# A graph attention kernel: one mask product in 16 bits, one product for three values an edge, and window tables with two buffers

## The reference, cut to what matters

```python
# x: (6250, 96) f32; src, dst: (200000,) int32, sorted by dst
q = (x[src] @ qW).reshape(e, 4, 24)
k = (x[dst] @ kW).reshape(e, 4, 24)
v = (x[dst] @ vW).reshape(e, 4, 24)
exp_s = exp(clip(sum(q * k, -1), -10, 10))
norms = segment_sum(exp_s, src)[src]
res = segment_sum((exp_s / (norms + 1e-8))[:, :, None] * v, src)
out = layernorm(x + (x + res))
```

## Time and profile before

| | |
|---|---|
| Median of 3 runs | 1709.44 us (1707.88 to 1710.03) |
| Profiled execution | 1711.48 us, its span 1709.3 us |
| Mean granted TensorE clock | 0.936 |
| Busy share of the span | PE 87%, VectorE (DVE) 86%, ScalarE (ACT) 74%, GpSimd (POOL) 59% |
| DMA | 465.03 MB, 272 GB/s over the span |
| Setup, first phase, second phase | to about 140, to about 856, to the end |

### The profile page before, as it was taken

The page is one execution under the profiler, slowest core; times in us unless marked ns, Lnnn a source line. Parts: engine busy times, 40 slices in busy tenths (PEclk is TensorE's granted clock), DMA queues, the critical chain, the costliest instruction groups (busy, mean ns, idle before and its releaser), DMA issues.

```text
span 1709.3 us, 56067 instructions
## 1 busy us (share of the span) xinstructions
PE 1482.0 (87%) x19964; PEld 1425.5 (83%) x19965; DVE 1469.3 (86%) x2980; ACT 1265.3 (74%) x1844; POOL 1016.7 (59%) x764
## 2 busy tenths in 40 slices
PE   4873988888888988888769999999999999999990
PEld 3652878888788878887759999999999999999990
DVE  6988998898988998898158999999999999999987
ACT  2341665565666666665559999999999999999984
POOL 6230776777777776777725555555555555555551
PEclk8566999999999999999979999999999999999995
DMA  5673899999999999999897777777777777777732
GB/s 155 225 276 132 312 370 337 336 346 366 348 352 343 341 367 339 357 339 344 333 302 257 238 238 241 244 238 239 239 243 242 237 240 240 243 239 237 240 113 56
DMA packets 159451, 465.03 MB, mean 272 GB/s; under 512 B 36994, under 2 KB 59266, under 8 KB 152244
## 3 DMA queue, kind: packets, MB, share of 16 engines
q1 hardware_dynamic: 123572, 301.16, 54.1%
q0 software_dynamic: 35840, 163.36, 23.9%
HBM read 271.21 MB, written 209.73 MB: 281 GB/s over the span
## 4 chain that ended last, share of the span: by engine, by line
PE 80%; DVE 8%; issue 6%; DMA 2%; SPq 2%; ACT 1%; POOL 0%; DVEq 0%; POOLq 0%; ACTq 0%
PE two_a L1131 14%; PE two_b L1131 13%; PE meta L1193 12%; PE sum_bank L1193 12%; PE two_a L1214 7%; PE two_b L1214 7%; PE one_d L1204 3%; PE one_c L1204 3%; PE meta L1149 2%; PE one_d L1160 2%; DMA work<-kv_table 1%; PE sum_bank L1113 1%; SPq L825 1%; DVE acc L1614 1%; DVE cols_work L1315 1%
## 5 line engine op out<-in xcount | busy, mean ns | idle before, releaser
L698 POOL TENSOR_TENSOR work<-work 128x768 f32<-128x768 f32 x236 | 450.8, 1910 | 357.4 <-ACT work L939 357.4
L635 POOL DMA_INDIRECT sorted_rows<-work x448 | 501.3, 1119 | 215.2 <-issue 215.2
L948 ACT ACTIVATE work<-work 128x1024 f32<-128x1024 bf16 x236 | 500.8, 2122 | 0.0
L1131 PE MATMUL two_a<-work 128*128 128x192 bf16 x2688 | 268.5, 251 | 86.8 <-issue 84.3
L903 ACT ACTIVATE work<-two_a 128x768 f32<-128x768 f32 x224 | 181.5, 810 | 187.0 <-PE two_a L1131 186.2
L1131 PEld LDWEIGHTS two_a<-work 128*128 128x128 f16 x2688 | 220.0, 100 | 107.5 <-issue 89.0
L1131 PE MATMUL two_b<-work 128*128 128x192 bf16 x2688 | 267.5, 251 | 0.0
L1193 PE MATMUL meta<-work 128*128 128x100 f32 x1888 | 236.1, 278 | 0.8 <-DVE acc L1548 0.8
L1193 PE MATMUL sum_bank<-work 128*128 128x100 f32 x1888 | 235.2, 278 | 0.0
L1579 DVE TENSOR_REDUCE work<-work 128x32 f32<-128x768 f32 x236 | 225.0, 953 | 8.2
L1131 PEld LDWEIGHTS two_b<-work 128*128 128x128 f16 x2688 | 225.9, 100 | 6.8
(11 more groups left out here) (229 smaller groups left out, 2211.8 us busy)
## 6 DMA issues: line engine op xcount, KB each, us to landing
work<-sorted_rows SPq DMA_DIRECT2D x472, 392.0 KB, 3.5
work<-sorted_local SPq DMA_DIRECT2D x56, 1024.0 KB
sorted_rows<-pad_rows SPq DMA_DIRECT2D x49, 392.0 KB, 4.5
work<-kv_table SPq DMA_DIRECT2D x112, 144.0 KB
sorted_rows<-work POOLq DMA_INDIRECT x448
kv_table<-work SPq DMA_DIRECT2D x12, 576.0 KB, 3.4
work<-in_x SPq DMA_DIRECT2D x12, 192.0 KB, 3.8
sorted_local<-work SPq DMA_DIRECT2D x56, 8.0 KB
```

The costliest lines, as they stand in the source:

```text
L635: pool.indirect_dma_start(out=rows_dram, out_offset=bass.IndirectOffsetOnAxis(ap=place_now[:, p, u, b:b + 1], axis=0), in_=payload[:, p, u ...
L698: pool.tensor_tensor(now[:, :, 0:D].rearrange("p c (h f) -> p c h f", h=HEADS), blk[:, k, :, :, D:2 * D].rearrange("p m c (h f) -> p (m c) ...
L948: act.activation(hot_f[:, k % HOTF], hot[:, k % HOTS].rearrange("p n c -> p c n"), ACT.Copy).then_inc(hotf_made[k % PSEM], 1)
L1131: mm = pe.matmul(to, picked[:, u % 2, k * P:(k + 1) * P], window[:, u, :, n, :], start=(n == 0), stop=(n == 2))
```

## The change

Three parts, in the functions of the first phase and of the setup.

1. **The mask.** ScalarE copies `slots` out of PSUM to 16 bits, spread to pairs (`slots_h`, 200 elements a partition), after its two copies of b and ahead of the copy of the turned targets. VectorE makes `masked` with one product of 1400 elements, both inputs 16 bits in SBUF. TensorE's next `first_slots` waits for ScalarE's copy, not for the mask.
2. **The values.** Three values an edge, not four: `src_tag`, `dst_hi`, `dst_lo`, held beside each other (`held`), and one product of 1344 elements makes `vals`. `dst_local` goes: the setup subtracts the base from the target itself, and the low part is the local target where the targets of a group span less than 128. The sort's products have 48 columns. The slow branch, not taken when every group's targets lie within one window, adds the base (`base_f`) back.
3. **The windows.** `window` has two buffers of both groups, and one semaphore for each buffer. The sync queue, at the head of each iteration, waits until `kv` of c - 1 is over for both groups and loads both windows for c + 1.

```diff
+        held = cols_work[:, 1:1 + NV, :] ... "p (g v c) -> p g v c", v=NV, c=HC)
+        src_tag, dst_hi, dst_lo = (held[:, :, v, :].rearrange("p (g h) c -> p g h c", h=HB) for v in range(NV))
-        window, at = share(at, [QUAD, 2, 3, D], BF16)
+        window, at = share(at, [2, QUAD, 2, 3, D], BF16)
# SyncE
-            def window_of(u, lo, at_c):
-                group_done(sp, kv_made[KPARTS - 1], u, at_c)
-                sp.dma_start(window[:, u].rearrange("p x a b -> p (x a b)"), kv3[bass.ds(lo, P), :]
-                             ).then_inc(window_in[u], 16)
+            def windows(los, p):
+                for u in range(QUAD):
+                    sp.dma_start(window[:, p, u].rearrange("p x a b -> p (x a b)"), kv3[bass.ds(los[u], P), :]
+                                 ).then_inc(window_in[p], 16)
 
             def emit(a, b, c, p=None):
+                if c is not None and (not isinstance(c, int) or c + 1 < NQ):
+                    p = parity(c, p)
+                    los, at_c = bases(plus(sp, c, 1)), counts(sp, c, G2, 0)
                     for u in range(QUAD):
-                        window_of(u, los[u], {})
+                        group_done(sp, kv_made[KPARTS - 1], u, at_c, 1)
+                    windows(los, 1 - p)
                 if b is not None:
                     ... (write local targets)
-                if c is not None and following:
-                    window_of(0, los[0], at_c)
                     ... (broadcast brow)
-                if c is not None and following:
-                    for u in range(1, QUAD):
-                        window_of(u, los[u], at_c)
# ScalarE
+                if a is not None:
+                    act.wait_ge(slots_made, plus(act, a, 1))
+                    if not zero(a):
+                        act.wait_ge(masked_made, a)
+                    act.activation(slots_h, slots.unsqueeze(3).to_broadcast([P, QUAD, NB, HC]), ACT.Copy
+                                   ).then_inc(slots_kept, 1)
# TensorE
-                    pe.wait_ge(window_in[u], c16)
+                    if u == 0:
+                        pe.wait_ge(window_in[p], loaded)
-                        pe.wait_ge(masked_made, times(pe, a, QUAD))
+                        pe.wait_ge(slots_kept, a)
# VectorE, setup
-            link(dve.tensor_tensor(dst_local, dcol_i, base_ps.unsqueeze(2).to_broadcast([P, NG, COLS]), ALU.subtract))
+            link(dve.tensor_tensor(dcol_i, dcol_i, base_ps.unsqueeze(2).to_broadcast([P, NG, COLS]), ALU.subtract))
+            link(dve.tensor_copy(base_f[:], base_ps))
-                link(dve.tensor_copy(dst_hi, bits))
+                link(dve.tensor_copy(dst_hi, pairs))
# VectorE, first phase
-                    for v, held in enumerate((src_tag, dst_hi, dst_lo, dst_local)):
-                        dve.tensor_tensor(vals[:, :, v], onej, quad_of(held, a).unsqueeze(2)
-                                          .to_broadcast([P, GH, NCH, HC]), ALU.mult).then_inc(vals_made, 1)
+                    dve.tensor_tensor(vals, onej.unsqueeze(2).to_broadcast([P, GH, NV, NCH, HC]),
+                                      held[:, bass.ds(times(dve, a, GH), GH)].unsqueeze(3)
+                                      .to_broadcast([P, GH, NV, NCH, HC]), ALU.mult).then_inc(vals_made, 1)
-                def mask(u):
-                    if u == 0:
-                        dve.wait_ge(slots_made, a1)
-                    dve.tensor_tensor(masked[:, HB * u:HB * (u + 1)], hits[:, 0, u],
-                                      slots[:, u, :].unsqueeze(1).unsqueeze(3).to_broadcast([P, HB, NB, HC]),
-                                      ALU.mult).then_inc(masked_made, 1)
+                def mask():
+                    dve.wait_ge(slots_kept, a1)
+                    dve.tensor_tensor(masked.rearrange("p (u h) t c -> p u h (t c)", u=QUAD),
+                                      hits[:, 0].rearrange("p u h t c -> p u h (t c)"),
+                                      slots_h.rearrange("p u t c -> p u (t c)").unsqueeze(2)
+                                      .to_broadcast([P, QUAD, HB, NB * HC]), ALU.mult).then_inc(masked_made, 1)
...
```

More of the change, by code:

```diff
@@ L95, in gnn_program @@
     AW = D + HEADS
-    NV = 4
-    TW = (NV - 1) * NCH
+    NV = 3
+    TW = NV * NCH
     TI = FULL_NT // TSLOT
@@ L156, in columns @@
             return cols_work[:, n, :].bitcast(F16).rearrange("p (g c) -> p g c", c=COLS)
-        src_tile, src_tag, dst_hi, dst_lo, dst_local, inner = (columns(n) for n in range(6))
+        src_tile, inner = columns(0), columns(5)
+        held = cols_work[:, 1:1 + NV, :].rearrange("p a b -> p (a b)").bitcast(F16).rearrange("p (g v c) -> p g v c", v=NV, c=HC)
+        src_tag, dst_hi, dst_lo = (held[:, :, v, :].rearrange("p (g h) c -> p g h c", h=HB) for v in range(NV))
         x_all = cols_work[:].rearrange("p a b -> p (a b)")[:, 0:NT * D].rearrange("p (t d) -> p t d", t=NT)
         run0 = sb("run0", [P, NG], F32)
+        base_f = sb("base_f", [P, NG], F32)
         slot0 = sb("slot0", [P, NG], F16)
@@ L212, in gnn_program @@
         masked, at = share(at, [GH, NB, HC], F16)
+        slots_h, at = share(at, [QUAD, NB, HC], F16)
         oneh, at = share(at, [GH, P, HC], F16)
@@ L661, in slow @@
                     pool.sem_inc(pool_turn, 1)
+                    pool.tensor_tensor(dst_part, dst_part, base_f[:, bass.ds(pool.snap(c * QUAD + u), 1)].to_broadcast([P, NCH]),
+                                       ALU.add).then_inc(slow_step, 1)
+                    pool.wait_ge(slow_step, made[1])
+                    pool.sem_inc(pool_turn, 1)
                     pool.tensor_copy(dst_now, dst_part).then_inc(slow_step, 1)
-                    pool.wait_ge(slow_step, made[1])
+                    pool.wait_ge(slow_step, made[2])
                     pool.sem_inc(pool_turn, 1)
@@ L675, in slow @@
                                            ).then_inc(slow_step, 1)
-                        pool.wait_ge(slow_step, made[2 * part + 2])
+                        pool.wait_ge(slow_step, made[2 * part + 3])
                         pool.tensor_tensor(to, to, far_rows[:, :, :, 2], ALU.add).then_inc(slow_step, 1)
-                        pool.wait_ge(slow_step, made[2 * part + 3])
+                        pool.wait_ge(slow_step, made[2 * part + 4])
                         pool.sem_inc(pool_turn, 1)
@@ L1102, in emit @@
                 if c is not None:
-                    done_c, c16 = counts(pe, c, G2, 1 - G2), times(pe, c, 16, 16)
+                    p = parity(c, p)
+                    done_c, loaded = counts(pe, c, G2, 1 - G2), times(pe, c, 8 * QUAD, 8 * QUAD * (2 - p))
                 def kv(u):
@@ L1274, in _ @@
             bits = edge_i.rearrange("p (g c) -> p g c", c=COLS)[:, 0:NG]
+            pairs = bits.rearrange("p g (h c) -> p g h c", c=HC)
             link(dve.tensor_scalar(bits, col_i, 7, LO - 1, ALU.logical_shift_right, ALU.bitwise_and))
@@ L1512, in emit @@
                 if a is not None:
-                    for u in range(QUAD):
-                        mask(u)
+                    mask()
                     slot_sums()
```

28 lines of the change are left out of this document (12 added, 16 removed).

## The result

The changed kernel takes 1732.51 us (1727.39 to 1735.58, 4 runs) against 1709.22 us of the kernel before (4 runs): a ratio of 1.0134, 95% interval 1.0108 to 1.016. I had forecast 1691 in a range to 1710. The profiled execution takes 1735.6 us, its span 1733.8. The last scatter starts at 880.1 us of the span, where it started at 855.9 before: those 24 us are the whole loss, all of it is in the sorting, and an iteration there takes 600 / 47.5 = 12.63 us (380 scatters in 200 to 800 us) where it took 12.24.

What follows compares the result with a forecast made beforehand. It took the window's ring, long because the DMA engines are full, to bound the sorting. Gains of 16.4 (windows) + 2.6 (first iterations) - 0.3 (setup) = 18.7 us from 1711.5 gave 1692.8, as median 1691 us; range 1667 to 1710.

Steps and rivals of the forecast that it cites:

- What bounds it: Sorting, 12.24 us an iteration: the window's ring ends PE's waits, with transfers at 11.75 us, POOL 11.42, VectorE 10.89 close behind.
- PE's ring: Sorting: window request to kv start 7.29 us, then 4.37 to the next request, a closed round of 11.66 us with one buffer.
- The windows: Sorting: two buffers end PE's 1.58 us wait; DMA share 0.985 saves 0.31 us an iteration, 16.4 us in all (0 to 84).
- Mask and values: VectorE in the sorting: mask 0.81 us less, values 0.45 us less an iteration, both worth 0 in the covered steady part.
- The mask and POOL: Sorting: scatters beside the new mask lengthen, POOL's demand rises from 11.42 to 11.67 us an iteration, 0 in the sum.
- First iterations: Before the first kv, nothing covers VectorE: three iterations each 0.86 us shorter, 2.6 us in all (1.0 to 4.0).
- Setup: Setup's chain: one more linked copy and copies into spread pairs cost 0.3 to 1.8 us, taken as 0.3.
- rival 1: Sorting: PE's window wait returns as ScalarE's wait for a free payload, period stays 12.24 us: 1707 us; chance 0.15 with Rival 5.
- Rival 4: Sorting: POOL's lock by the new mask lengthens scatters, the period grows 0.3 us, 1723 us; chance 0.11.
- Rival 5: Sorting: the wait at kv isn't the window's, so the outcome is as rival 1, 1707 us; chance 0.15 with rival 1.

Runs made afterwards that it cites:

- h7: The kernel before with two window buffers and the write of the local targets ahead of the window loads: 1697.25 us, ratio 0.9935.
- e1: The changed kernel with the windows' old single buffers and old places on the sync queue, leaving mask and values: 1705.35 us, ratio 0.999 to the kernel before.
- e3: The changed kernel with the write of the local targets moved ahead of the window loads on the sync queue: 1698.36 us, ratio 0.9947 to the kernel before.
- g3: The same kernel as e3 (changed kernel, write ahead of the window loads) on another chip: 1698.83 us, ratio 0.9935 to the kernel before.
- g5: The changed kernel with the write of the local targets on ScalarE's queue and four buffers in HBM: 1697.01 us, ratio 0.9926 to the kernel before.
- g8: The changed kernel with the write ahead of the window loads and the old mask, merged values kept: 1695.19 us, ratio 0.9913 to the kernel before.
- g9: The changed kernel with the write ahead of the window loads and the new mask's product made twice: 1702.85 us, ratio 0.9967 to the kernel before.
- h1: The changed kernel with the write on ScalarE's queue and the old mask, two window buffers and merged values kept: 1693.66 us, ratio 0.9917 to the kernel before.
- e8: The same kernel as g8 (write first, old mask, merged values) on a chip where the kernel before took 2013.49 us: 2020.6 us.
- f8: The same kernel as g8 (write first, old mask, merged values) on a chip where the kernel before took 2025.31 us: 2022.44 us.
- e5: The same kernel as g5 (write on ScalarE's queue) on a chip where the kernel before took 2013.49 us: 2072.6 us.
- e9: The same kernel as g9 (write first, new mask's product twice) on a chip where the kernel before took 2013.49 us: 1959.67 us.
- f5: The same kernel as g5 (write on ScalarE's queue) on a chip where the kernel before took 2025.31 us: 2086.77 us.
- f9: The same kernel as g9 (write first, new mask's product twice) on a chip where the kernel before took 2025.31 us: 1958.23 us.
- e7: The same kernel as h7 (kernel before, two window buffers, write first) on a chip where the kernel before took 2013.49 us: 2010.32 us.

## Why the prediction was wrong, point by point

- **What bounds it**: right in what it read, short in what it left out. PE's ring, the transfers' 11.75 us, POOL's 11.42 and VectorE's 10.89 were the near limits. The sync queue was not among them: I had used its window requests alone, not its order of waits. There 6.3 us in the mean passed from the write to the next broadcast, in part in SP's waits for PE (324.8 us in all), which left 1.6 us an iteration (79.4 us) to be seen as waiting for the landing. The change took the cover away.
- **The windows, the step that failed**: "so no wait is lengthened, but 288 KB more stand in front of an 8 KB write: at 349 GB/s under 0.9 us. `brow` made from it is used two iterations later. I take 0." Three things are wrong in it. The time from write to broadcast grew by 3.1 us in the iterations shown and by 3.3 in the mean, not by 0.9: I had let the 288 KB move at the full 349 GB/s, and in the iteration above they moved at about 75 GB/s beside the scatters (0.30 MB in 4 us), 3.9 us by that rate. The slack of two iterations belongs to the data of `brow`, not to the queue: SP waits for the landing in place, and what is behind it, windows too, waits along. And ScalarE can't copy the next turned targets (L931, 93 us) until the write has landed, `kv` copies standing behind it. The term was +0.31 us an iteration in favour; measured 0.39 against.
- **The size of the windows' term** fits the other order: with the write first, h7 runs at 11.94 us an iteration against 11.93 forecast. That is in part luck. The DMA share there is 0.97, not 0.985, and the transfer work 0.97 x 11.94 = 11.6 us, not the 11.75 that I held fixed. The kernel gains 10.9 us where that rate would give 0.30 x 53 = 15.9. In the profiled executions the stretch from first to last scatter is 15.7 us shorter (176.7 to 841.4 us, 175.5 to 855.9 before), as the rate gives; the first scatter starts 1.2 us later, and what lies behind the last one, unchanged code, takes 858.3 us where it took 853.4 (850.7 to 856.2 in e1, e3, g3, g5, g8, g9 and h1). Why that part differs is open.
- **Mask and values**: right. 886, 858 and 337 ns against 878, 850 and 340, and worth nothing that can be told from no change while covered (e1: 0.9976 to 1.0004).
- **The mask and POOL**: I took 0.35 us an iteration less 0.10 for the shorter values product, 0.25 in all. g3 against g8 gives 8 x 0.040 = 0.32 us for the mask alone; mask and values together, e1 against the kernel before, give 8 x 0.071 = 0.57 (a scatter takes 1195 ns after 1124), twice what I took. That it cost nothing (e1) was forecast. g9 shows that the reason (a lock of so much for each such product) isn't right. The rule of the Trainium skill (SBUF — State Buffer, "Who interferes with whom"), by which a VectorE instruction with two inputs in SBUF contends with GpSimd's reads, agrees with g8 against g3 in sign; that a second one beside it adds nothing, it doesn't explain. The prediction says that the rule leaves open whether a scatter's descriptors count; the same section of the Trainium skill infers that making descriptors needs the write side, which such an instruction leaves free. By that inference the scatters should not have lengthened at all.
- **First iterations**: the masks of the changed kernel stand 9.59 us apart, 0.85 less where 0.86 was forecast, but the first scatter starts at 175.3 us after 175.5, so the 2.6 us don't arrive there; with the write first it starts at 173.9 (g3). By this one start they can't be judged: in e8, f8 and g8, one kernel on three chips, it lies between 174.2 and 176.7. From the chain of the changed kernel:

```profile
148.85 0.90 DVE work L1493
...
158.44 0.90 DVE work L1493
```

- **Setup**: the copies into pairs stay as fast (0.99 us each), the added copy is 0.29, as forecast.

```profile
53.99 0.29 DVE base_f L1311
...
63.25 0.99 DVE cols_work L1319
```

- **Rivals**: rival 1 named the wait that comes next, ScalarE's for a free `payload`. It is 148.3 us in g3, and PE's wait is 85.5 us after 77.6, behind ScalarE now; but the period falls all the same, to 12.0 us. Rival 4 named the other side, by POOL's lock, at 1723; the sign came true by another mechanism, and e1 refutes the named one as its cause. Rival 5 comes nearest: the wait at `kv` was the window's, but a second buffer doesn't remove it when the queue that has to ask for the load is itself late.

## What to carry to other kernels

A queue that waits in order for the landing of its own transfer is an engine like the others: add up its ring (issues, the transfers ahead of the one waited for, the landing) before moving anything on it, however small the bytes. On the chips where this kernel takes 1708 us it paid to put the small transfer that something waits for ahead of the large ones that nobody needs yet, or on another queue; a second buffer helps only if the request is really made earlier. And where a step on such a queue is moved, ask which wait has so far covered the landing.

## What the runs showed of the hardware that I hadn't expected

- An 8 KB write to HBM, issued in the mean 6.6 to 6.7 us behind a 1 MB broadcast, takes 4.6 to 6.0 us from issue to the step that waits for it, 5.3 to 5.5 in the mean, while the DMA engines are 96 to 97% busy (g3, h7), even alone in its queue (g5). Issued in the mean 3.2 us behind the broadcast, with two windows of 144 KB between them, it takes 6.6 to 11.6, 9.6 in the mean (the changed kernel).
- In the iteration looked at, the two windows, 288 KB, went at about 75 GB/s while the scatters had 73 to 88% of the engines' time, a fifth of the 337 GB/s that the changed kernel moves in all.
- PE's granted clock in the sorting is 0.97 before, 0.92 in the changed kernel and 0.99 to 1.00 in every kernel with the write first or on ScalarE's queue (e3, g3, g5, g8, g9, h1, h7), although PE waits 85.5 us there (g3, for ScalarE): more waiting than before's 77.6 us, and yet the full clock, 2.4 GHz. The waits of the changed kernel for its windows last up to 3.0 us, those before up to 2.8, those of g3 up to 2.1. What of this sets the clock is not shown.
- On two chips (e5 to e9, f5 to f9) these kernels take 15 to 23% longer than on the others, the kernel before 18%, and in the profiles it is in the sorting: in e7 the last scatter starts at 1164.8 us, and the part behind it, 851.8 us, is no longer than elsewhere.
